# Moving weight-quantiser units between the stages of a fused two-layer kernel, and reordering each unit's steps

## The chip, the cores and the metric

One core of one Trainium2 chip. The metric is the device time of one execution in microseconds (us); lower is better. An execution before the change takes 3158.2 us (median of 3 runs, 3157.79 to 3158.3). Engines: PE multiplies matrices (PEld is its weight load), ACT is ScalarE, DVE is VectorE, POOL is GpSimd, SP issues all DMAs.

## What is computed

Two transformer layers on x (2 x 512 x 1024) with a context (2 x 1024 x 1024), in float32. Every matrix product is done as three products of high and low halves, so each operand is first split in two.

```
x = x + attention(norm(x), context)           # 32 query heads, 8 key heads, rotary, mask, projection wo
x = x + router(norm(x))                       # softmax of 64 logits, top 8, a mix of 64 bias rows
x = x + fake_quant(norm(x)) @ fake_quant(context)
x = x + w3' (silu(w1' norm(x)) * (w2' norm(x)))   # w1, w2 2752 x 1024, w3 1024 x 2752
```

w1', w2', w3' are the weights after a 4-bit quantiser: each block of 64 numbers is divided by its largest absolute value, each quotient goes to the nearest of 16 code values, and the result is multiplied back.

## The kernel before, in words

**Quantiser units.** The three weights are cut into 65 units of 128 x 1024 numbers (two are smaller), and the units are worked off beside the matrix products of four stages, on DVE, ACT and GpSimd. One unit (class Nf4): SP loads it; DVE takes the blocks' maxima and their reciprocals (max_vector, L212 to L219); GpSimd multiplies by the reciprocals (norm_gpsimd, L224); then come numbered steps. In steps 0 to 6 ACT makes a steep Relu of the normalised numbers into one of two ramp buffers (L241) and DVE adds its clipped value to the running code (L262 for step 0, else L265). In step 7 DVE subtracts the code from the numbers (L268); step 8 is empty. In step 9 ACT takes the Sign of that difference (L245) and then the first of three Prelu folds of the code (L250), steps 10 and 11 are the other folds, and after step 11 DVE makes the two final operations (L271, L273). GpSimd multiplies by the maxima (finish_gpsimd, L278) and SP stores the unit to DRAM. So NS4, the steps of a unit, is 12. Relu j waits for DVE's step j - 2, because there are two ramp buffers; the folds live in the second of them.

**Spread** (L295) gives a stage's units to its slots: the steps of all units in a row are shared out in proportion to a weight per slot. The next unit's maximum is due with step 8 of the one before (ahead), its normalisation `lag` slots later; the finish `lag` slots after the last step, the store `sync_lag` slots after that. In the front ACT and DVE do a step in the same slot; in the other stages DVE does it one slot later.

**Which units go where** (build, L2113): 34 in the front stage, 12 in attention (AT), 8 beside the projection (o_units, spread1), 11 beside the gate and down products (f_units, spread2). `chunks` counts the 128-row chunks of w1 and w2 that are quantised before the tail stage, `late_units` the units beside the projection.

**Front** (L350): keys, values and queries. 128 tiles of 24 matmuls each, with transposes between; four PSUM banks. Of a rotated tile ACT copies the result (L608), DVE makes the sine part (L658, L659), GpSimd the cosine part and the sum (L728, L731). For each pair of tiles ACT makes the high half of the next weights (L591) and GpSimd the low half (L714), two tiles ahead. Each engine works through its slot in a written order: on GpSimd the low half, then units' norms and finishes, then the rotation.

**Attention** (L821): 256 steps of scores, softmax, transposes and mixing; a unit has some 20 steps of time.

**Tail** (L1374): first the projection, 128 heads ("head" slots) of 12 matmuls; ACT splits off the high half of a head's ring buffer (L1634), GpSimd (even heads, L1912) or DVE (odd heads, L1736) the low half; SP loads a head four slots ahead. Beside it the context is turned into codes: ACT scales (L1639), GpSimd clips (L1916), DVE rounds by adding and subtracting a large constant (L1751). A second chain (class Chain) carries the router and the code product of each half of the tokens as links with hand-written slot offsets r, z, y from a base slot (64 and 128): for example z is the slot of ACT's scaling, then DVE's rounding (L1846), PE's transposes of the codes (L2060), ACT's copy, the product (L2064); y are the last transposes (L2046). Then come the gate and up products ("gate" slots, 12 matmuls) and the down products ("down" slots, twice 6 matmuls into two alternating PSUM banks that DVE adds to x, L1776). Weights of the next items are turned by PE (L2021), split by ACT (L1652) and DVE (L1764). Units of spread2 run from slot 179 to slot 337 of 392.

**SP's order at the start of the tail:** heads 0 and 1, four scales, heads 2 and 3, units 0 and 1, contexts 0 and 1, the router's weight, the expert bias, the router's bias; then slot by slot. DVE waits for the scales and for the router's three loads before its first low half:

```
            dve.wait_ge(k_ready, 1)
            dve.wait_ge(ro_in, 48)
            low(1)
            for q in range(TOTAL + 2):
```

## Time and profile before

| | us |
|---|---|
| median of 3 runs | 3158.2 |
| the profiled execution | 3158.93 |
| its span, first to last instruction | 3157.2 |
| PE busy | 2954.9 (94%) |
| DVE busy | 2311.9 (73%) |
| ACT busy | 1919.0 (61%) |
| POOL busy | 1094.0 (35%) |

The granted TensorE clock is 0.979 of full speed over the span. Busy time of PE is a union of matmuls that overlap, so it says less than the distance from one start to the next. A row of waits says who stood, whose end released it, the total in us, how often and the longest. A row of a window gives the busy time of each engine in that stretch with the count of instructions in brackets.

### The profile page before, as it was taken

The numbers are of one execution on the slowest core, as the hardware profiler recorded it, in microseconds if no ns is written. First come the engines' busy times: TensorE is split into PE (matmuls) and PEld (weight loads), VectorE is DVE, ScalarE is ACT, GpSimd is POOL, SyncE is SP. The second block draws the span as 40 slices with busy tenths as digits, with TensorE's granted clock in tenths as the row PEclk, the third lists the DMA queues.
The fourth block names the chain that finished last, engine by engine and source line by source line (L and its number), as shares of the span: only waits on it lengthen the run. The fifth ranks groups of instructions, "written<-read, shape, count | busy, mean of one in ns | idle before, by whom it ended". The sixth has DMA issues, their size and how long they took to land. (4 is left out here: it accounts for less than half of the span.)

```text
span 3157.2 us, 39853 instructions
## 1 busy us (share of the span) xinstructions
PE 2954.9 (94%) x14326; PEld 2414.3 (76%) x14336; DVE 2311.9 (73%) x3394; ACT 1919.0 (61%) x2643; POOL 1094.0 (35%) x644
## 2 busy tenths in 40 slices
PE   7989899989799999999999978998999999999999
PEld 6767687767588888888888856776786788888887
DVE  5878788788588888888888748788456666666633
ACT  4676666666488888888888756655343344444411
POOL 4626428777623333333333246543300000000000
PEclk9999999999899999999999989999999999999999
DMA  5445344343332222222222187743421232222111
GB/s 181 143 151 169 120 136 134 114 137 127 125 109 83 79 94 84 78 94 81 88 101 73 55 301 261 242 166 132 169 67 61 85 96 87 74 72 67 60 37 57
DMA packets 231108, 362.18 MB, mean 115 GB/s; under 512 B 19456, under 2 KB 114688, under 8 KB 230912
## 3 DMA queue, kind: packets, MB, share of 16 engines
q1 hardware_dynamic: 230912, 359.63, 34.4%
q8 instruction: 115, 1.88, 0.2%
q14 instruction: 81, 0.66, 0.1%
HBM read 266.90 MB, written 92.67 MB: 114 GB/s over the span
## 5 line engine op out<-in xcount | busy, mean ns | idle before, releaser
L1108 DVE CUSTOM_DVE_ANT_0 at_sc<-at_s,at_mk 128x1024 f32<-128x1024 f32 x256 | 312.0, 1219 | 100.6 <-issue 98.2
L132 PE MATMUL fr_acc<-fr_xh,fr_wh 128*128 128x512 f32 x768 | 308.8, 402 | 57.6 <-POOL fr_wl L714 52.4
L241 ACT ACTIVATE fr_nf_above<-fr_nf_raw,sharp 128x1024 f32<-128x1024 f32 (+1 forms) x238 | 258.8, 1103 | 164.6 <-POOL fr_nf_raw L224 107.0
L1123 DVE TENSOR_TENSOR at_ptl<-at_t,at_pth 128x512 fp32r<-128x512 f32 x512 | 326.5, 679 | 30.6 <-ACT at_pth L1070 30.6
L1070 ACT ACTIVATE at_pth<-at_t 128x512 fp32r<-128x512 f32 x512 | 277.4, 595 | 112.0 <-PE at_t L1170 111.3
L1060 ACT ACTIVATE at_pr<-at_sc,at_low 128x1024 f32<-128x1024 f32 x256 | 295.7, 1155 | 36.0 <-DVE at_low L1108 30.6
L133 PE MATMUL fr_acc<-fr_xl,fr_wh 128*128 128x512 f32 x768 | 305.4, 398 | 0.0
L134 PE MATMUL fr_acc<-fr_xh,fr_wl 128*128 128x512 f32 x768 | 305.0, 397 | 0.0
L1170 PE MATMUL at_t<-ident,at_pr 128*128 128x128 f32 x2048 | 267.8, 273 | 12.2 <-DVE at_ptl L1123 11.2
L1170 PEld LDWEIGHTS at_t<-ident,at_pr 128*128 128x128 f32 x2048 | 236.3, 140 | 53.9 <-issue 19.3
L265 DVE SCALAR_TENSOR_TENSOR fr_nf_val<-fr_nf_above,fr_nf_val 128x1024 f32<-128x1024 f32 (+1 forms) x204 | 246.5, 1209 | 20.4 <-ACT fr_nf_above L241 3.2
L132 PE MATMUL tl_pa<-tl_ring_h 128*128 128x512 f32 x512 | 210.0, 410 | 40.9 <-POOL tl_ring_l L1912 16.1
L1912 POOL TENSOR_TENSOR tl_ring_l<-tl_ring,tl_ring_h 128x1024 fp32r<-128x1024 f32 x64 | 162.5, 2539 | 193.6 <-ACT tl_ring_h L1634 193.5
L132 PEld LDWEIGHTS fr_acc<-fr_xh,fr_wh 128*128 128x128 f32 x768 | 148.4, 193 | 99.3 <-issue 58.0
L132 PE MATMUL at_o<-at_pth,at_vh 128*128 128x512 f32 x512 | 221.9, 433 | 0.2 <-DVE at_ptl L1123 0.2
L132 PE MATMUL at_s<-at_kh,at_qh 128*128 128x512 f32 x512 | 201.8, 394 | 11.8 <-POOL at_ql L1004 11.8
L1652 ACT ACTIVATE tl_gu<-tl_pt 128x512 fp32r<-128x512 f32 x120 | 71.7, 597 | 226.5 <-PE tl_pt L2021 226.5
L1764 DVE TENSOR_TENSOR tl_gu<-tl_pt,tl_gu 128x512 fp32r<-128x512 f32 x120 | 82.6, 688 | 169.8 <-ACT tl_gu L1652 169.2
L133 PE MATMUL tl_pa<-tl_ring_l,tl_ring_h 128*128 128x512 f32 x512 | 203.9, 398 | 0.0
L134 PE MATMUL tl_pa<-tl_ring_h,tl_ring_l 128*128 128x512 f32 x512 | 203.6, 398 | 0.0
L134 PE MATMUL at_s<-at_kh,at_ql 128*128 128x512 f32 x512 | 201.9, 394 | 0.0
L134 PE MATMUL at_o<-at_pth,at_vl 128*128 128x512 f32 x512 | 201.1, 393 | 0.0
(224 smaller groups left out, 7842.6 us busy)
## 6 DMA issues: line engine op xcount, KB each, us to landing
tl_raw<-dq SPq DMA_DIRECT2D x87, 512.0 KB, 3.6
tl_ring<-o_d SPq DMA_DIRECT2D x128, 256.0 KB, 3.2
tl_ring<-in_L_xattn_wo SPq DMA_DIRECT2D x128, 256.0 KB, 3.9
fr_nf_raw<-in_L_ffn_w SPq DMA_DIRECT2D x33, 512.0 KB, 3.6
dq<-fr_nf_val SPq DMA_DIRECT2D x33, 512.0 KB, 3.6
fr_raw<-in_L_xattn_wq SPq DMA_DIRECT2D x32, 512.0 KB, 4.5
q_d<-fr_res SPq DMA_DIRECT2D x64, 256.0 KB, 2.3
rows<-q_d SPq DMA_DIRECT2D x64, 256.0 KB, 2.7
```

Source lines behind the costliest of these rows:

```text
L132: pe.matmul(out, w[0], x[0], start=start, stop=False)
L133: pe.matmul(out, w[0], x[1], start=False, stop=False)
L134: return pe.matmul(out, w[1], x[0], start=False, stop=stop)
L241: act.activation(self.ramps[j % 2][:, w], x, ACT.Relu, bias=self.sharp[:, j:j + 1], scale=SHARP).then_inc(self.above_done.sem, 1)
L265: dve.scalar_tensor_tensor(v, above, STEPS[j], v, ALU.min, ALU.add).then_inc(self.stepped.sem, 1)
L1060: act.activation(pr[:, n % 2], sc[:, n % 2], ACT.Exp, bias=low[:, n % 2:n % 2 + 1], scale=-1.0, accum_out=sums[:, h % 2, quarter:quarter + ...
L1070: act.activation(pt[0][:, h % 2, j * HALF:(j + 1) * HALF, (n % QT) * P:(n % QT + 1) * P], t_ps[:, j], ACT.Copy).then_inc(t_hi.sem, 1)
L1108: dve.tensor_tensor_reduce(sc[:, n % 2], s_ps[:, n % 2], mk[:, bb * QT + n % QT], -1.0, -NEG, ALU.add, ALU.min, low[:, n % 2:n % 2 + 1]).t ...
L1123: dve.tensor_tensor(pt[1][sl], t_ps[:, j], f32(pt[0][sl]), ALU.subtract).then_inc(t_lo.sem, 1)
L1170: last = pe.transpose(t_ps[:, j, c, :], pr[:, n % 2, k * P:(k + 1) * P], ident[:])
L1764: dve.tensor_tensor(lo, pt[:, no % 2], f32(hi), ALU.subtract).then_inc(w_lo, 1)
L1912: pool.tensor_tensor(ring_l[:, q % 4], ring[:, q % 4], f32(ring_h[:, q % 4]), ALU.subtract).then_inc(ring_lo_p, 1)
```

## The change

The units go to 28 / 12 / 2 / 23 over the four stages. The empty step goes (11 steps): the folds follow directly on the seventh step, Sign comes last. Outside attention DVE trails ACT by one step instead of one slot (or none). The next unit's maximum is due with step 5. GpSimd does a slot's finishes ahead of its norms. In the projection the context's rounding becomes an ACT operation that adds the constant, a GpSimd clip in the shifted numbers and an ACT operation that subtracts it; the contexts come two slots later; loads at the stage's start are put into later slots; DVE's wait for the router's loads moves to slot 62. Some links of the second chain move by a slot. Beside the gate and down products, a gate slot has weight 1 and a down slot 0.3.

```diff
-NS4 = NP4 + len(FOLDS) + 2
+AHEAD = 5
+NS4 = NP4 + len(FOLDS) + 1

     def above_scalar(self, act, n, s, steps, width=D):
...
-            f = j - NP4 - 2
-            if j < NP4:
+            f = j - NP4
+            if f < 0:
...
-            if f == 0:
+            elif f < len(FOLDS):
+                scale, _, slope = FOLDS[f]
+                if f:
+                    act.wait_ge(self.above_done.sem, n * NA4 + NP4 + f)
+                else:
+                    act.wait_ge(self.stepped.sem, n * ND4 + 2 * ND4 + NP4)
+                act.activation(fold, fold if f else self.val[:, s, w], ACT.Prelu, ...)
+            else:
                 act.wait_ge(self.stepped.sem, n * ND4 + 2 * ND4 + NP4 + 1)
                 act.activation(x, x, ACT.Sign, ...)
-            if f >= 0:
-                scale, _, slope = FOLDS[f]
-                if f:
-                    act.wait_ge(self.above_done.sem, n * NA4 + NP4 + 1 + f)
-                act.activation(fold, fold if f else self.val[:, s, w], ACT.Prelu, ...)

 class Spread:
-    def __init__(self, units, weights, lag=1, sync_lag=1, ahead=8):
+    def __init__(self, units, weights, lag=1, sync_lag=1, ahead=AHEAD, norm_lag=1):
...
                 where[divmod(k, NS4)] = q
+                if k:
+                    self.late[q].append(divmod(k - 1, NS4))
+        self.late[where[divmod(total - 1, NS4)] + 1].append(divmod(total - 1, NS4))
...
-                self.norms[where[u - 1, ahead] + lag].append(u)
+                self.norms[where[u - 1, ahead] + norm_lag].append(u)

 front_stage
-        plan = Spread(len(units), [...])
+        plan = Spread(len(units), [...], lag=1, sync_lag=2)
-                for u, j in plan.steps[q]:
+                for u, j in plan.late[q]:
                     nf.step_vector(dve, u, u % 2, [j], parts[u], units[u][2])
-                    if j == 8 and u + 1 < len(units):
+                    if j == AHEAD and u + 1 < len(units):
                         nf.max_vector(dve, u + 1, ...)
...
+                for u in plan.finishes[q]:
+                    nf.finish_gpsimd(pool, u, u % 2, units[u][2])
                 for u in plan.norms[q]:
                     nf.norm_gpsimd(pool, u, u % 2, units[u][2])
-                for u in plan.finishes[q]:
-                    nf.finish_gpsimd(pool, u, u % 2, units[u][2])

 attention_stage
-        plan = Spread(len(units), [n >= UNITS_FROM for n in range(ALL - 4)], lag=2, sync_lag=6)
+        plan = Spread(len(units), [n >= UNITS_FROM for n in range(ALL - 4)], lag=2, sync_lag=6, norm_lag=2)
-                    if j == 8 and u + 1 < len(units):
+                    if j == AHEAD and u + 1 < len(units):

 Chain._batch
-        r, z, y = ..., [43 + t for t in range(QT)]
+        r, z, y = ..., [44 + t for t in range(QT)]
-        for n, (var, root) in enumerate(((2, 3), (24, 25), (40, 41))):
+        for n, (var, root) in enumerate(((2, 3), (24, 25), (41, 42))):
-                    put("dve", r[t] + 9 if n == 1 else z[t] + 4, "stats", t, n)
+                    put("dve", r[t] + 9 if n == 1 else z[t] + 5, "stats", t, n)
-                put("pe", z[t] + 2, "product", t, h)
-                put("dve", z[t] + 3, "product", t, h)
+                put("pe", z[t] + 3, "product", t, h)
+                put("dve", z[t] + 4, "product", t, h)
-            put("pe", z[t] + 1, "codes", t)
-            put("act", z[t] + 2, "codes", t)
+            put("pe", z[t] + 2, "codes", t)
+            put("act", z[t] + 3, "codes", t)

 tail_stage
-            return 1.0
+            return 1.0 if s[0] == "gate" else 0.3
-        spread1 = Spread(len(o_units), [...], lag=2, sync_lag=2)
-        spread2 = Spread(len(f_units), [...], lag=2, sync_lag=2)
+        spread1 = Spread(len(o_units), [...], lag=1, sync_lag=2)
+        spread2 = Spread(len(f_units), [...], lag=1, sync_lag=2)
+        CONTEXT_FROM = 5
         def context_slot(n):
-            return 3 + 3 * n
+            return CONTEXT_FROM + 3 * n
+        def x_slot(t):
+            return 14 + 3 * t if t < QT else 34 + 5 * t
 sync
-            for q in range(2):
+            for q in range(4):
                 load_head(q)
-            for j, v in enumerate(scales):
-                sp.dma_start(par[:, j:j + 1], ...).then_inc(par_in, 16)
-            for q in range(2, 4):
-                load_head(q)
-            for u in range(2):
-                nf1.load_early_sync(sp, u, u, o_units[u][0])
-            for n in range(2):
-                load_context(n)
-            sp.dma_start(rw, router_w).then_inc(ro_in, 16)
-            sp.dma_start(eb[:], expert_b).then_inc(ro_in, 16)
-            sp.dma_start(rb, ...).then_inc(ro_in, 16)
+            nf1.load_early_sync(sp, 0, 0, o_units[0][0])
             for q in range(TOTAL + 2):
                 if q + 4 < FIRST:
                     load_head(q + 4)
-                if 4 <= q < 4 + TT:
-                    sp.dma_start(X[:, q - 4, :], ...)
+                if q == 0:
+                    for j, v in enumerate(scales):
+                        sp.dma_start(par[:, j:j + 1], ...).then_inc(par_in, 16)
+                if q == 1:
+                    nf1.load_early_sync(sp, 1, 1, o_units[1][0])
+                if q in (2, 4):
+                    load_context(q // 2 - 1)
+                if q == 40:
+                    sp.dma_start(rw, router_w).then_inc(ro_in, 16)
+                    sp.dma_start(eb[:], expert_b).then_inc(ro_in, 16)
+                    sp.dma_start(rb, ...).then_inc(ro_in, 16)
+                for t in range(TT):
+                    if q == x_slot(t):
+                        sp.dma_start(X[:, t, :], x_tiles[t]).then_inc(x_in[t], 16)
                 for n in range(NC):
-                    if q == context_slot(n) + 2:
+                    if q == context_slot(n) + 4:
                         store_context(n)
                         if n + 2 < NC:
                             load_context(n + 2)
 scalar
+            def round_context(n):
+                act.wait_ge(ones_made, 1)
+                act.wait_ge(ctx_scaled, n + 1)
+                act.activation(rows[:, n % 2], rows[:, n % 2], ACT.Identity, bias=rounding[:, 0:1]).then_inc(ctx_rounded, 1)
+            def code_context(n):
+                act.wait_ge(ctx_clipped, n + 1)
+                if n >= 2:
+                    act.wait_ge(ctx_out[n % 2], 16 * (n // 2))
+                act.activation(codes[:, n % 2], rows[:, n % 2], ACT.Identity, bias=rounding[:, 1:2]).then_inc(ctx_coded, 1)
...
                     if q == context_slot(n):
                         scale_context(n)
+                    if q == context_slot(n) + 1:
+                        round_context(n)
+                    if q == context_slot(n) + 3:
+                        code_context(n)
 vector
-            def round_context(n):
-                dve.wait_ge(ctx_clipped, n + 1)
...
-            dve.wait_ge(par_in, 64)
...
-            dve.wait_ge(ro_in, 48)
             low(1)
             for q in range(TOTAL + 2):
+                if q == CONTEXT_FROM - 1:
+                    constants()
+                if q == plan.BASE[0] - 2:
+                    dve.wait_ge(ro_in, 48)
...
-                for u, j in of1(spread1.steps, q - 1):
+                for u, j in of1(spread1.late, q):
...
-                for u, j in of2(spread2.steps, q - 1):
+                for u, j in of2(spread2.late, q):
 gpsimd
-                pool.tensor_scalar(rows[:, n % 2], rows[:, n % 2], QMAX, 0.0, ALU.min, ALU.max).then_inc(ctx_clipped, 1)
+                pool.tensor_scalar(rows[:, n % 2], rows[:, n % 2], ROUND + QMAX, ROUND, ALU.min, ALU.max).then_inc(ctx_clipped, 1)
-                    if q == context_slot(n):
+                    if q == context_slot(n) + 2:
                         clip_context(n)
...

 build
-    chunks, late_units = 12, 8
+    chunks, late_units = 9, 2
```

## Rows read from the trace of the kernel before

**Rows 1.** The page's first line: the span and the instructions.

```profile
span 3157.2 us, 39853 instructions
```

**Rows 2.** Busy time by stage, core 0; columns as in the first line.

```profile
core 0: us, PE busy (x) PEld busy (x) DVE busy (x) ACT busy (x) POOL busy (x), PEclk, DMA share, GB/s
...
6.40:851.80 845.40, 753.19 (x3264) 612.27 (x3264) 662.15 (x722) 541.21 (x607) 509.95 (x309) 0.96 0.42 138
...
863.50:1813.00 949.50, 936.95 (x5120) 787.37 (x5120) 804.16 (x1564) 791.08 (x1314) 297.49 (x181) 1.00 0.26 87
...
1825.10:2287.00 461.90, 415.63 (x1830) 324.66 (x1836) 338.41 (x364) 264.38 (x278) 224.70 (x99) 0.95 0.62 213
2287.00:2497.00 210.00, 198.44 (x1017) 154.71 (x1022) 132.41 (x252) 73.68 (x118) 4.18 (x4) 0.98 0.21 63
2497.00:2990.00 493.00, 488.74 (x2347) 401.80 (x2346) 311.25 (x399) 217.74 (x280) 40.04 (x21) 1.00 0.25 78
```

**Rows 3.** PE in order of time in the front: start us, us, instruction.

```profile
700.00 0.39 PE L132 MATMUL fr_acc<-fr_xh,fr_wh 128*128 128x512 f32 x1
...
706.35 0.39 PE L133 MATMUL fr_acc<-fr_xl,fr_wh 128*128 128x512 f32 x1
```

**Rows 4.** What PE waited for in the front: us, times, longest.

```profile
PE fr_acc L132 <- POOL fr_wl L714: 52.4, 21, 7.3
PE fr_acc L764 <- DVE rows L670: 15.1, 1, 15.1
PE fr_acc L132 <- POOL fr_vl L720: 10.9, 1, 10.9
```

**Rows 5.** Waits of ACT and DVE in the front, same columns, whole span.

```profile
ACT fr_nf_above L241 <- POOL fr_nf_raw L224: 107.0, 25, 8.2
...
ACT fr_nf_raw L245 <- DVE fr_nf_raw L268: 94.6, 33, 5.5
...
DVE fr_nf_val L262 <- ACT fr_nf_above L241: 64.0, 22, 6.8
```

**Rows 6.** Busy time of each engine over the front's query tiles.

```profile
600.00:850.00 250.00, 216.76 (x900) 174.75 (x899) 197.72 (x205) 154.98 (x167) 182.81 (x115) 0.95 0.37 120
```

**Rows 7.** DVE in order of time in the front: three steps in a row.

```profile
703.97 3.88 DVE L265 SCALAR_TENSOR_TENSOR fr_nf_val<-fr_nf_above,fr_nf_val 128x1024 f32<-128x1024 f32 x3
```

**Rows 8.** What PE waited for in attention.

```profile
PE at_t L1170 <- DVE at_ptl L1123: 11.2, 12, 1.6
```

**Rows 9.** DVE in order of time in attention, at a unit's end.

```profile
1052.50 2.19 DVE L273 TENSOR_TENSOR at_nf_val<-at_nf_above,at_nf_val 128x1024 f32<-128x1024 f32 x1
```

**Rows 10.** What PE waited for in the projection (1813 to 2290).

```profile
PE tl_pa L132 <- POOL tl_ring_l L1912: 16.1, 5, 12.2
PE tl_pa L132 <- DVE tl_ring_l L1736: 15.9, 5, 11.3
PE tl_pa L132 <- DVE tl_X L1745: 9.2, 4, 7.3
PE tl_pc L2060 <- DVE tl_two L1846: 8.6, 3, 4.2
PE tl_pc L2046 <- DVE tl_yT L1862: 4.5, 1, 4.5
```

**Rows 11.** Order of time at the projection's start; in brackets the idle time before.

```profile
1840.28 2.36 DVE L1736 TENSOR_TENSOR tl_ring_l<-tl_ring,tl_ring_h 128x1024 fp32r<-128x1024 f32 x2 [14.96 <-DMA tl_two<-in_L_ffn_router_bias]
```

**Rows 12.** A group of ACT by line, 1815 to 2300: busy us, mean ns, idle before.

```profile
L1639 ACT ACTIVATE tl_rows<-tl_rows,tl_two 128x1024 f32<-128x1024 f32 x16 | 19.7, 1230 | 0.0
```

**Rows 13.** Busy time on the units' tile alone, gate stretch.

```profile
2497.00:2990.00 493.00, 0.00 (x0) 0.00 (x0) 142.29 (x119) 134.56 (x119) 40.04 (x21) 1.00 0.25 78
```

**Rows 14.** Groups of DVE by line, gate stretch.

```profile
L265 DVE SCALAR_TENSOR_TENSOR tl_two<-tl_two 128x1024 f32<-128x1024 f32 x66 | 80.3, 1217 | 0.9 <-ACT tl_two L241 0.3
...
L262 DVE TENSOR_SCALAR tl_two<-tl_two 128x1024 f32<-128x1024 f32 x11 | 11.6, 1056 | 0.0
```

**Rows 15.** The unit's first step on DVE in attention, by line.

```profile
L262 DVE TENSOR_SCALAR at_nf_val<-at_nf_above 128x1024 f32<-128x1024 f32 x12 | 8.2, 683 | 0.0
```

More of the change, by code:

```diff
@@ L308, in __init__ @@
         self.units, self.slots = units, slots
-        self.steps, self.maxes, self.norms, self.finishes, self.loads, self.stores = (
-            [[] for _ in range(slots)] for _ in range(6))
+        self.steps, self.late, self.maxes, self.norms, self.finishes, self.loads, self.stores = (
+            [[] for _ in range(slots)] for _ in range(7))
         where = {}
@@ L486, in weight @@
             return w
-        plan = Spread(len(units), [weight(kind, n) for kind, n, _ in ORDER])
+        plan = Spread(len(units), [weight(kind, n) for kind, n, _ in ORDER], lag=1, sync_lag=2)
         slot_of = {(kind, n, half): q for q, (kind, n, half) in enumerate(ORDER)}
@@ L1324, in _batch @@
             self._put("dve", columns_at + h + 1, "columns", b, 0, h)
-        r, z, y = [6 + 3 * t for t in range(QT)], [27 + 3 * t for t in range(QT)], [43 + t for t in range(QT)]
+        r, z, y = [6 + 3 * t for t in range(QT)], [27 + 3 * t for t in range(QT)], [44 + t for t in range(QT)]
         for t in range(QT):
             put("dve", 1 + t // 2, "stats", t, 0)
-        for n, (var, root) in enumerate(((2, 3), (24, 25), (40, 41))):
+        for n, (var, root) in enumerate(((2, 3), (24, 25), (41, 42))):
             put("act", root, "root", 0, n)
@@ L1446, in tail_stage @@
         ones = two[:, 5952:6016].bitcast(BF16)
+        rounding = words(two, 6016, 2)
         nf1 = Nf4(make_tools(ctx, nc, "t1"), sharp, buffers=nf1_buffers)
@@ L1482, in weight2 @@
                 return 0.0
-            return 1.0
-        spread1 = Spread(len(o_units), [weight1(q) for q in range(FIRST)], lag=2, sync_lag=2)
-        spread2 = Spread(len(f_units), [weight2(q) for q in range(TOTAL)], lag=2, sync_lag=2)
+            return 1.0 if s[0] == "gate" else 0.3
+        spread1 = Spread(len(o_units), [weight1(q) for q in range(FIRST)], lag=1, sync_lag=2)
+        spread2 = Spread(len(f_units), [weight2(q) for q in range(TOTAL)], lag=1, sync_lag=2)
         parts1, parts2 = ([sum(len(us[v][0]) for v in range(u % 2, u, 2)) for u in range(len(us))]
@@ L1745, in add_heads @@
                     dve.tensor_tensor(X[sl], pa[:, t], X[sl], ALU.add).then_inc(o_added, 1)
-            def round_context(n):
-                dve.wait_ge(ctx_clipped, n + 1)
-                if n >= 2:
-                    dve.wait_ge(ctx_out[n % 2], 16 * (n // 2))
-                dve.tensor_scalar(codes[:, n % 2], rows[:, n % 2], ROUND, ROUND + QMID, ALU.add, ALU.subtract).then_inc(ctx_coded, 1)
             def product(i, j):
@@ L1893, in _ @@
                     hidden_low(i, j)
-                for n in range(NC):
-                    if q == context_slot(n) + 1:
-                        round_context(n)
                 for kind, b, t, h in chain.due("dve", q):
                     link(kind, b, t, h)
-                for u, j in of1(spread1.steps, q - 1):
+                for u, j in of1(spread1.late, q):
                     nf1.step_vector(dve, u, u % 2, [j], parts1[u])
-                    if j == NP4 and u + 1 < len(o_units):
+                    if j == AHEAD and u + 1 < len(o_units):
                         nf1.max_vector(dve, u + 1, (u + 1) % 2, parts1[u + 1], parts=len(o_units[u + 1][0]))
-                for u, j in of2(spread2.steps, q - 1):
+                for u, j in of2(spread2.late, q):
                     nf2.step_vector(dve, u, u % 2, [j], parts2[u])
-                    if j == NP4 and u + 1 < len(f_units):
+                    if j == AHEAD and u + 1 < len(f_units):
                         nf2.max_vector(dve, u + 1, (u + 1) % 2, parts2[u + 1], parts=len(f_units[u + 1][0]))
@@ L1950, in _ @@
                     pool.tensor_scalar(xn[:, t % 2], xn[:, t % 2], QMAX, 0.0, ALU.min, ALU.max).then_inc(c_clip, 1)
+                for u in of1(spread1.finishes, q):
+                    nf1.finish_gpsimd(pool, u, u % 2)
                 for u in of1(spread1.norms, q):
                     nf1.norm_gpsimd(pool, u, u % 2)
[L1953 to L1954 removed]
+                for u in of2(spread2.finishes, q):
+                    nf2.finish_gpsimd(pool, u, u % 2)
                 for u in of2(spread2.norms, q):
                     nf2.norm_gpsimd(pool, u, u % 2)
[L1957 to L1958 removed]
         @block.tensor
```

36 lines of the change are left out of this document (18 added, 18 removed).

## Prediction

> **What bounds the kernel now.** The profiled execution took 3158.93 us, 0.73 above the median of 3158.2; its span is 3157.2 us [rows 1], and 1.7 us lie around it. I cut the span into its stages first [rows 2]: the front (6.4 to 851.8), attention (863.5 to 1813), the projection (1825.1 to 2287), the first gate items with the second token batch's side chain (to 2497), the gate items that carry quantiser units (to 2990), the end. PE is busy nearly everywhere, so each stage has to be held against PE's own pace. Where PE lacks nothing its matmuls start 6.35 us / 28 = 0.227 us apart [rows 3]. The front's 3072 such matmuls need 697 us and its 192 transposes some 21 (the 3264 in its row), 718 of 845.4: it loses 127 us. Attention is at its pace but for a few us. The unit-carrying gate stretch has PE busy 488.7 of 493. So the money is in the front and in the projection, and the gate stretch has nothing to give.
>
> What PE waits for there: in the front 52.4 us in 21 waits for GpSimd's low halves of the weights, one wait of 15.1 for DVE's normalised rows, one of 10.9 for GpSimd's low half of the value weights [rows 4]. The rest of the 127 is start-up and the clock: 0.96 granted on average, so part of the stage at the lower of its two levels (1.2 GHz), against 1.00 in attention [rows 2]. GpSimd is only where it surfaces. In the front ACT stood 107.0 us for the unit's normalisation and 94.6 for DVE's subtraction ahead of Sign, DVE 64.0 for the first Relu of a unit [rows 5]: the three engines stop each other at each unit's start and end, and the low half queues in order behind that. From 600 to 850, 900 matmuls are 37.5 tiles; per tile DVE was busy 197.7/37.5 = 5.27 us, GpSimd 4.87, ACT 4.13, and PE at its pace needs 24 x 0.227 = 5.45 [rows 6]. DVE would have to be 97% busy with no wait; it has waits, so PE has.
>
> **The change, part by part.** Units (65 in all) go from 34/12/8/11 to 28/12/2/23. A unit's instructions are unchanged; their order, the lag of DVE behind ACT and the empty twelfth step change.
>
> *Front, six units fewer.* Consecutive DVE steps start 3.88/3 = 1.29 us apart [rows 7]; a unit has 11 long ones (two of them the end, one the maximum) and two short, 14.3 us. With 3.1 of 12 steps per tile, units are 3.6 of the 5.27; times 28/34 that is 3.0, so DVE falls to 4.67, 86% of PE's 5.45. Steps per full query tile fall from 3.2 to 2.4. The stalls go too: the next unit's maximum moves from step 8 to step 5, with three more steps for GpSimd's normalisation (the 107.0 and the 64.0); the folds read the finished value at once and Sign comes last, after DVE has long subtracted (the 94.6); DVE trails by one step within the slot. What is late next is the end of a unit (Relu 1 shares the folds' buffer, so ACT waits about two DVE steps), and a load that is issued a slot later with its maximum sooner: about 2.5 slots for a transfer, absorbed by the four accumulator banks. Of the 52.4 I take 42, of the 15.1 13, of the 10.9 8 and 5 of the small waits: 68, and with them 15 of the 29 us that clock and unlisted gaps cost. **Front -83** (bounds -35, where GpSimd's 4.87 of 5.45 stays the limit, and -105, all but start-up).
>
> *Attention.* Same units, same lag; but the maximum now shares a slot with a step. PE already has 12 waits, 11.2 us, for DVE here, one per unit [rows 8], where a unit's end holds DVE (2.19 us for the last sum [rows 9]). A maximum plus a step is 3.0 us against 3.4 there, so a second, smaller wait per unit: **+4** (0 to +12).
>
> *Projection.* PE waits for both kinds of low halves 16.1 + 15.9 (12.2 of it the stage's first load, which stays), 9.2 at sweep ends, 8.6 for the rounded codes, 4.5 for the last transposes [rows 10]. After the first head PE stands because DVE's first low half sits behind the router bias, the last of the start's loads: 14.96 us of idle DVE [rows 11]. That wait moves to slot 62, its three loads to slot 40, ten slots ahead of their use; x tiles spread out, and unit 1 and the contexts are issued behind head loads and no longer ahead of them. Six units leave DVE (86 us), ACT (6 x 12.4 = 74) and GpSimd. The 16 context roundings leave DVE; ACT gets 32 operations like its scaling, 1.23 us each [rows 12], 39 us, less than the 74 that left it, within PE's three heads per context. If that cover goes, ACT's splits are late, up to +10. SP now holds head loads behind a context's code, but four slots ahead of PE. The codes get one slot more, which covers the 8.6. Of 42 us of waits that can go I take 36, and 10 of the half-clock (0.95 here). **Projection -46** (-25 to -60).
>
> *Second side chain.* Codes: -3. But the last transposes come a slot later and now border on the first gate that reads them: 0 to 4.5 (the row of the same wait [rows 10]), I take 4. **+1.**
>
> *Gate stretch, twelve units more.* In 493 us the units' own tile took DVE 142.3 us and ACT 134.6 [rows 13]; DVE was busy 311.3 in all [rows 2], so 164 after some 5 us of short unit work is other work. Now 164 + 5 (issue) + 23 x 14.3 = 498 of 493, 101%. ACT: 217.7 - 134.6 + 23 x 12.4 = 368, 75%. DVE becomes the bound. Weights 1 for gate slots and 0.3 for down slots put two steps in a gate slot: with 164/158 us of other work per slot about 3.6 us of DVE, against PE's 493/158 = 3.1. So DVE is 2 to 5 us behind when a down group starts, and there PE has two banks and can only cover some 1.5 us: it stands 1 to 3.5 us at each of 14 groups, 2 on average: 28 us. Queued behind late steps are DVE's adds, the low halves of weights (slack of two slots) and, on SP, weight loads behind the units' stores (slack of ten). GpSimd gets 24 more operations. In this stretch DVE's two-input step takes 1217 ns and its only slowed form is the unit's first step, 1056 [rows 14] against 683 in attention [rows 15]; 11 x 0.37 is 4 us beside 21 GpSimd operations, and I take as much for the 24 more. Of 28 + 4 a lagging DVE makes up some 2 in the slots after the last unit: **gate +30.** Below: +5, the bare excess of DVE's sum, if backlog is spread perfectly. Above: +110, if DVE gets no further than the 79% at which it was busy while it held PE up in the front (198 of 250 [rows 6]; busy alone its work is 164 + 23 x 13.6 = 477, and 477/0.79 = 603). Today PE idles 4.3 us here [rows 2] and DVE's steps hardly wait, so I stay nearer to the lower end.
>
> The Trainium skill, "SBUF — State Buffer", section "SBUF: two separate sides", says that VectorE operations with two SBUF inputs and GpSimd operations exclude each other on a shared port pair for a whole instruction. Attention's 2.19 us sum beside a GpSimd subtraction looks like it, the 1217 ns steps of the gate stretch do not. By the page every added GpSimd operation could block DVE for its length, which would put about 46 us in place of my 4 and the sum near 3106.
>
> **Sum:** -83 + 4 - 46 + 1 + 30 = -94; 3158.9 - 94 = 3065 for a profiled execution, 3064 us for the median.
>
> **Rivals.** (a) *The gate stretch hides it*, +5, and the front gives 95: 3027. For: ACT and GpSimd have room. Against: 101%. (b) *GpSimd keeps the front*: -35, so 3112. For: PE's waits name it, 89% per tile. Against: it idles on the waits that go. (c) *GpSimd blocks DVE in the gate stretch*: operations that met DVE's idle time now meet work, and each of the 24 stops DVE for its own length, 40.04/21 = 1.9 us [rows 13]: 46 in place of 4, so 3106. For: the 2.19 us row. Against: the 1217. The Trainium skill's page named above would have this one. (d) *Slower*: in the gate stretch Relu, step and fold stop each other as they do in the front, with PE directly behind DVE's adds at every down group. Its 477 us of DVE work at the projection's busy share of 338/462 = 73% [rows 2] take 651, +158 in place of +30: 3192. It decides from a share below 77% (477/617: then it eats the other stages' 124). That counts are not what the change says is no rival: they follow from two constants.
>
> **How the numbers follow.** Forecast 0.54 (3040 to 3095), (a) 0.15, (b) 0.12, (c) 0.10, (d) 0.09. The range 3015 to 3125 holds the forecast, (a), (b), (c) with their mixed bounds and leaves (d) and double mishaps out. A measurement of this kernel can tell about 0.2%, 6 us. Slower: (d) with a little, 0.10; the same: (b) and (c) together with a gate stretch at +60, 0.05; faster 0.85.
>
> **What would show it.** Front: PE's wait for the weights' low half under 15 us, the 107.0, 94.6 and 64.0 mostly gone, end near 770. Projection: no wait for the router bias, none for the codes; about 415 us long. Gate stretch: DVE above 44 of 50 busy, PE's waits for DVE's adds some 25 to 30 us in about 14 or more pieces. Wrong if the front still ends after 810, if the gate stretch grows by over 60 us, or if its waits sit on weights' low halves in place of the adds.

## The result and the profile after

After the change a run takes 3212.35 us (median of 4, 3211.61 to 3216.21) against 3158.25 (median of 4, 3157.79 to 3160.53): a ratio of 1.0166, 95% interval 1.0154 to 1.0179. The change makes the kernel 54 us slower; 94 us faster was forecast.

The windows of the profile after, cut at the first and last matmul of each stage: front, attention, projection, the rest of the side chain, the gate stretch up to the quantiser's last instruction, the end. The columns are those of [rows 2].

```profile
core 0: us, PE busy (x) PEld busy (x) DVE busy (x) ACT busy (x) POOL busy (x), PEclk, DMA share, GB/s
6.40:756.10 749.70, 730.29 (x3264) 603.80 (x3264) 577.16 (x644) 470.64 (x541) 491.24 (x298) 0.99 0.45 147
767.10:1732.60 965.50, 940.50 (x5120) 786.31 (x5120) 811.72 (x1564) 792.58 (x1313) 303.08 (x181) 1.00 0.25 85
1744.70:2192.10 447.40, 414.94 (x1836) 325.76 (x1836) 225.51 (x273) 230.59 (x245) 195.51 (x87) 0.96 0.60 205
2192.10:2398.10 206.00, 196.69 (x1023) 153.39 (x1023) 131.60 (x252) 71.08 (x115) 4.17 (x4) 0.99 0.21 64
2398.10:3050.10 652.00, 541.26 (x2383) 433.89 (x2382) 487.76 (x561) 364.46 (x419) 100.60 (x46) 0.92 0.25 79
```

The last row decides. The kernel before, cut in the same way, has this one (a little wider than the last of [rows 2]):

```profile
2493.90:2997.70 503.80, 499.54 (x2397) 410.69 (x2396) 317.89 (x408) 223.09 (x287) 41.93 (x22) 1.00 0.25 79
```

and PE waited in it, but for small gaps, for DVE's adds alone:

```profile
PE tl_pa L132 <- DVE tl_X L1776: 4.2, 5, 1.3
```

So the gate stretch grew by 148 us. DVE is busy in 487.8 of 652 us, 75%. PE's busy time grew by 42 us for no more matmuls: the granted clock fell from 1.00 to 0.92 in the stretch, so part of it ran at the lower of the two levels, 1.2 GHz. The rest of the 148 is PE standing. What PE waited for after the change, by stage (front, attention, projection, gate stretch), in us, times, longest; the line numbers are those of the kernel after:

```profile
PE fr_acc L133 <- POOL fr_wl L720: 5.4, 1, 5.4
...
PE at_t L1176 <- DVE at_ptl L1129: 23.8, 23, 2.4
...
PE tl_pa L133 <- POOL tl_ring_l L1938: 24.7, 4, 12.1
PE tl_pa L133 <- DVE tl_X L1775: 8.8, 4, 5.3
PE tl_pc L2074 <- DVE tl_two L1841: 7.2, 1, 7.2
...
PE tl_pa L133 <- DVE tl_X L1800: 64.5, 15, 7.9
PE tl_pt L2049 <- DVE tl_gu L1788: 35.3, 16, 4.6
PE tl_pa L133 <- DVE tl_dn L1788: 8.1, 5, 4.6
```

The front's 52.4 us [rows 4] are down to 5.4; attention's 12 waits [rows 8] are 23; in the projection GpSimd's low halves cost more than before [rows 10]; and in the gate stretch PE stands 64.5 + 35.3 + 8.1 = 108 us for DVE (its adds at L1800, the weights' low halves at L1788), where it was idle for some 4 before. What ACT and DVE waited for in that stretch:

```profile
ACT tl_two L250 <- DVE tl_two L268: 106.1, 23, 14.0
ACT tl_two L242 <- DVE tl_two L268: 68.1, 57, 6.9
ACT tl_two L242 <- DVE tl_two L276: 47.1, 17, 12.5
...
DVE tl_gu L1788 <- ACT tl_gu L1678: 59.6, 53, 4.3
DVE tl_X L1800 <- PE tl_pa L135: 49.7, 49, 2.4
DVE tl_dn L1788 <- ACT tl_dn L1678: 24.4, 19, 5.2
```

These waits form a ring. ACT's Relus and folds (L242, L250) wait for DVE's steps (L268; L276 is a unit's last sum), with the weights' high halves queued behind them; DVE waits for those high halves (L1678) and for PE's sums, with its steps queued behind; PE waits for DVE. Every engine has idle time, and none can use it.

### The profile page after: what moved, and what is told of

It reads as the page before. It is cut to its first block and busy times, and to the rows that moved or that the text cites. A ratio compares the mean times of both kernels' runs of the same rounds, so it can differ in the third digit from the quotient of the medians.

```text
span 3210.8 us, 39903 instructions
## 1 busy us (share of the span) xinstructions
PE 2979.2 (93%) x14336; PEld 2431.1 (76%) x14336; DVE 2291.4 (71%) x3378; ACT 1956.0 (61%) x2675; POOL 1108.9 (35%) x646
## 5 line engine op out<-in xcount | busy, mean ns | idle before, releaser
L133 PE MATMUL fr_acc<-fr_xh,fr_wh 128*128 128x512 f32 x768 | 300.9, 392 | 7.1 <-POOL fr_wl L720 5.4
L242 ACT ACTIVATE fr_nf_above<-fr_nf_raw,sharp 128x1024 f32<-128x1024 f32 (+1 forms) x196 | 215.9, 1102 | 114.7 <-DVE fr_nf_val L268 53.2
L242 ACT ACTIVATE tl_two<-tl_two,sharp 128x1024 f32<-128x1024 f32 x161 | 184.4, 1148 | 124.9 <-DVE tl_two L268 68.1
L1766 DVE TENSOR_TENSOR tl_ring_l<-tl_ring,tl_ring_h 128x1024 fp32r<-128x1024 f32 x64 | 92.4, 1444 | 198.4 <-ACT tl_ring_h L1649 198.3
L133 PE MATMUL tl_pa<-tl_dn,tl_hT 128*128 128x512 f32 x352 | 155.9, 443 | 80.9 <-DVE tl_X L1800 69.2
L268 DVE SCALAR_TENSOR_TENSOR fr_nf_val<-fr_nf_above,fr_nf_val 128x1024 f32<-128x1024 f32 (+1 forms) x168 | 201.3, 1198 | 13.7 <-ACT fr_nf_above L242 3.0
L1649 ACT ACTIVATE tl_ring_h<-tl_ring 128x1024 fp32r<-128x1024 f32 x128 | 133.9, 1053 | 124.1 <-PE tl_pa L135 79.2
```

Of the source, the lines that this page charges most:

```text
L133: pe.matmul(out, w[0], x[0], start=start, stop=False)
L242: act.activation(self.ramps[j % 2][:, w], x, ACT.Relu, bias=self.sharp[:, j:j + 1], scale=SHARP).then_inc(self.above_done.sem, 1)
L268: dve.scalar_tensor_tensor(v, above, STEPS[j], v, ALU.min, ALU.add).then_inc(self.stepped.sem, 1)
L1649: act.activation(ring_h[:, q % 4], ring[:, q % 4], ACT.Copy).then_inc(ring_hi, 1)
```

## The experiments

The theories of the gate stretch's loss. **A**: 23 units are too much work for DVE beside its evictions (the operations that take PE's results out of PSUM). **B**: the new order locks ACT and DVE together (a fold waits for DVE's step of the same slot). **C**: the weights 1 and 0.3 bunch the steps. Two more came after x1 to x4. **B'**: a unit's chain alternates between ACT and DVE in either order and sets the pace. **Port**: DVE and GpSimd stop each other.

Each of these kernels but x12 ran once. A stage whose code several of them share tells how much one run can say: with the new order and 28 units the front took 746.5 to 750.9 us in seven runs, the projection with the change's own code 447.4 to 450.2 in three, so a difference under some 5 us in a stage says little.

**x1: the new order, the old units.** "Order" stands here and below for all of the change but the number of units: the steps' order, the codes, the loads' places, the side chain's slots and the slots' weights.

```diff
-    chunks, late_units = 9, 2
+    chunks, late_units = 12, 8
```

> The new order of steps and the new placing of the context codes, but the units as they were before: 34 in the front, 12 in attention, 8 in the projection, 11 in the gate stretch. Theory A (amount: in the gate stretch VectorE has too much to do for 23 units beside the evictions): with 11 units the gate stretch is back at 493 us within 15, although the order is the new one. Theory B (lockstep: a fold on ScalarE waits for VectorE's step of the same slot, and both queues are in order): the stretch stays over 510 us with 11 units. By both the front comes to 800 to 850 us (A: 845, since the six units that left it made the gain; B: below 820, since there the order itself made part of it) and the projection to 450 to 500 us. Total 3140 to 3200 us.

3212.6 us, beside 3161.8 for the kernel before in the same session. **x2: the old order, the new units** is the kernel before with one line changed:

```diff
-    chunks, late_units = 12, 8
+    chunks, late_units = 9, 2
```

> The kernel before in every line but the numbers of units: 28/12/2/23, with the old order of steps, the old lags, the context codes as they were, and the gate stretch's steps spread evenly over its slots. A (amount): gate stretch 620 to 670 us as with the new order. B (lockstep of the new order): below 590 us. A third, C (the weights 1 and 0.3 of gate and down slots bunch the steps): also below 600 us, since here they lie evenly, and then a run of the change with even weights tells B from C. Front 760 to 800 us if the six units alone make its gain, projection 400 to 430 us.

3159.9 us. The two halves of the change are now apart (us, stages cut as above; the whole is the median for the kernel before and after, one run for x1 and x2):

| order, units | front | attention | projection | side chain | gate stretch | whole |
|---|---|---|---|---|---|---|
| old, 34/12/8/11 (before) | 845.4 | 949.4 | 461.7 | 207.1 | 503.8 | 3158.3 |
| new, 34/12/8/11 (x1) | 845.6 | 967.7 | 494.3 | 205.9 | 506.5 | 3212.6 |
| old, 28/12/2/23 (x2) | 740.8 | 950.0 | 417.0 | 207.2 | 653.7 | 3159.9 |
| new, 28/12/2/23 (after) | 749.7 | 965.5 | 447.4 | 206.0 | 652.0 | 3212.4 |

The units alone, in the old order: -104.6 in the front (more than the 45 to 85 that I had written down), -44.7 in the projection, +149.9 in the gate stretch, together nothing. The order alone, with the old units and with the new: 0 and +9 in the front, +18 and +16 in attention, +33 and +30 in the projection, +3 and -2 in the gate stretch; with the side chain's -1 these make 53 and 52 us, nearly the whole loss of 54. B falls, since 11 units in the new order take 506.5 and 23 in the old one 653.7; C falls, since x2's steps are evenly spread. A is left, and a chain through both engines that is as long in either order, B'.

These are x2's stretch, and what PE waited for in it:

```profile
2344.70:2998.40 653.70, 541.79 (x2399) 434.13 (x2398) 473.62 (x565) 365.94 (x419) 91.85 (x46) 0.93 0.26 80
```

```profile
PE tl_pa L132 <- DVE tl_X L1776: 82.0, 22, 7.9
PE tl_pt L2021 <- DVE tl_gu L1764: 26.3, 15, 3.7
```

The ring is there in the old order too: in x2's stretch ACT waits 91.2 us for DVE's steps, 71.1 for its subtraction and 62.7 for a unit's last sum, 225 in all beside 221 in the change. With 11 units in the old order the same three were 20.2, 5.7 and 12.6.

**x3: VectorE's steps halved. x4: ScalarE's steps halved.** In the gate stretch alone:

```diff
-                    nf2.step_vector(dve, u, u % 2, [j], parts2[u])
+                    nf2.step_vector(dve, u, u % 2, [j], parts2[u], D if j == 0 else 512)     # x3
-                    nf2.above_scalar(act, u, u % 2, [j])
+                    nf2.above_scalar(act, u, u % 2, [j], D if j < 2 else 512)                # x4
```

> The change, but in the gate stretch's 23 units VectorE's later steps (all but the first of a unit) work on half the columns, as does its subtraction and its two last operations; the other half of these units' values is left wrong. The waits are all kept. This takes about 23 x 9 operations x 0.6 us = 125 us off VectorE in the stretch (487 to about 365 us) and nothing off ScalarE. A (VectorE is the bound): the stretch gives back most of the 125 us and stands at 530 to 560 us. B (lockstep: a cycle through both engines): it gives back about the same, since the chain is shorter by as much. Told apart only together with the next run, in which ScalarE's work is halved instead.

> The change, but in the gate stretch's 23 units ScalarE's steps (from the third of a unit on: ramps, folds, sign) work on half the columns; the other half of these units' values is left wrong. The waits are all kept. This takes about 23 x 9 x 0.5 us = 105 us off ScalarE in the stretch (365 to about 260 us) and nothing off VectorE. A (VectorE is the bound): the stretch moves by less than 20 us. B (lockstep): it gives back over 50 us, to below 600 us.

The gate stretch of x3, then of x4:

```profile
2403.50:2972.10 568.60, 520.85 (x2384) 421.16 (x2383) 377.47 (x562) 362.75 (x419) 95.88 (x46) 0.96 0.29 91
```

```profile
2400.30:3006.70 606.40, 521.71 (x2383) 418.98 (x2382) 487.69 (x561) 278.64 (x419) 100.57 (x46) 0.96 0.27 85
```

DVE lost 110 us of work and the stretch 83; ACT lost 86 and the stretch 46. That is more than the 20 that A allows for ACT and less than B's 50, and x3's 568.6 is above A's 560. A chain through both engines is at work, and since the order plays no part, it is B' or a mixture with A.

**x5: no waits between the two engines** in these 23 units, with an edit in attention and one in the projection.

```diff
     # gate stretch, VectorE: the unit itself (raw) in place of ScalarE's ramps; no wait for above_done
-    dve.scalar_tensor_tensor(v, above, STEPS[j], v, ALU.min, ALU.add)
+    dve.scalar_tensor_tensor(v, x, STEPS[j], v, ALU.min, ALU.add)
     # gate stretch, ScalarE: the first fold reads raw; Relu and Sign wait for ScalarE's own results alone
-    # attention and projection
-        plan = Spread(..., lag=2, sync_lag=6, norm_lag=2)
-                    if j == AHEAD and u + 1 < len(units):
+        plan = Spread(..., lag=2, sync_lag=6, ahead=8, norm_lag=2)
+                    if j == 8 and u + 1 < len(units):
-        spread1 = Spread(..., lag=1, sync_lag=2)
+        spread1 = Spread(..., lag=1, sync_lag=2, norm_lag=6)
```

> The change with one edit in each of three stages, each to be read from its own stage. Gate stretch: ScalarE and VectorE do the same number of operations of the same sizes for the 23 units, but VectorE reads the unit itself instead of ScalarE's result and ScalarE the unit instead of VectorE's, so neither waits for the other in the quantiser (these units' values are therefore not the quantiser's). Theory A (the amount of work on VectorE): the stretch stays at 630 to 655 us. Theory B' (the chain of a unit that alternates between the two engines, 652/23 = 28.3 us a unit with the old order and with the new, so 17 units or so would go into a stretch of 500): the stretch falls below 580 us with the same busy times. Attention: the next unit's maximum is taken at VectorE's empty step 8 instead of with step 5; if the +17 us of the new order there come from that place, attention is back at 950 us within 4, else it stays at 966. Projection: GpSimd takes the second unit's normalisation six slots after the maximum instead of one; if GpSimd's standing before it costs the matmuls what its wait is, the projection loses 8 to 14 us of its 447, else under 4.

**x6: the codes back on VectorE, GpSimd nearly idle in the gate stretch.**

```diff
-    pool.tensor_scalar(rows, rows, ROUND + QMAX, ROUND, ALU.min, ALU.max)         # slot + 2
+    pool.tensor_scalar(rows, rows, QMAX, 0.0, ALU.min, ALU.max)                   # the scaling's slot
-    round_context, code_context on ScalarE (slot + 1, slot + 3), store at slot + 4
+    dve.tensor_scalar(codes, rows, ROUND, ROUND + QMID, ALU.add, ALU.subtract)    # slot + 1, store at slot + 2
-    nf2.finish_gpsimd(pool, u, u % 2), nf2.norm_gpsimd(pool, u, u % 2)
+    nf2.finish_gpsimd(pool, u, u % 2, BLK), nf2.norm_gpsimd(pool, u, u % 2, BLK)
```

> The change with an edit in each of two stages. Projection: the context codes are made as before (ScalarE scales, GpSimd clips in the same slot, VectorE rounds one slot later, stored two slots later); the units stay at two. The old order and old codes with two units took 417 us there, the new order and new codes 447: if the codes make the difference, the projection comes to 415 to 425 us, if GpSimd's wait for the second unit's maximum or the new order of loads does, it stays over 435. Gate stretch: GpSimd's normalisation and finish of the 23 units work on 64 of 1024 columns (the other columns stay unscaled), which takes nearly all of its 100 us away. Theory port (VectorE and GpSimd stop each other there): the stretch falls by 40 us or more; A or B': by less than 15 us.

The gate stretch of x5, then the projection and the gate stretch of x6:

```profile
2379.90:2968.70 588.80, 523.41 (x2383) 420.94 (x2382) 496.26 (x561) 361.38 (x419) 100.62 (x46) 0.96 0.27 88
```

```profile
1744.50:2177.80 433.30, 408.58 (x1836) 322.46 (x1836) 247.44 (x289) 199.01 (x213) 188.00 (x87) 0.97 0.62 212
2388.30:3013.30 625.00, 531.13 (x2381) 425.79 (x2379) 462.17 (x561) 364.41 (x419) 28.14 (x46) 0.94 0.27 83
```

Gate stretch: -63 us without the waits, though DVE was busy for 8.5 us more, so the chain is real, but 588.8 is above the 580 of B' and far below A's 630: neither alone. GpSimd: -27, between the two limits written down, and DVE's busy time fell by nearly as much (487.8 to 462.2). DVE's steps (L268) of the change and of x6, in ns min/median/max, show how:

```profile
L268 DVE SCALAR_TENSOR_TENSOR tl_two<-tl_two x138: 1160/1224/2605, 2417.2 to 3039.8; 128x1024 f32<-128x1024 f32 x138
```

```profile
L268 DVE SCALAR_TENSOR_TENSOR tl_two<-tl_two x138: 1160/1219/1228, 2407.5 to 3004.6; 128x1024 f32<-128x1024 f32 x138
```

Most steps run freely; 13 of the 138 take 2.0 to 2.6 us, each begun while a GpSimd operation ran, and with GpSimd nearly idle none does.

Attention came to 954.7 us in x5 with 15 waits (13.9 us) in place of 23; with the same edit it took 950.6 in x9 and 951.2 in x13, so the maximum beside a step is nearly all of the 16 us. In the projection the late normalisation gave 6 us and the codes on DVE 14. Both lie between the limits written down for a cause and for none, so neither is the whole of the 30.

**x9: the edits of x5 and x6 together. x13:** x9 with VectorE's later steps in the gate stretch on 512 columns, the second side chain's slots as before (z + 1, z + 2, y = 43, ...) and `lag=2` in spread1.

> The change with the edits of x5 and x6 together: in the gate stretch no waits between ScalarE and VectorE in the 23 units and GpSimd on 64 of 1024 columns (values not the quantiser's, most columns unscaled), in attention the maximum at the empty step, in the projection the codes as before and the normalisation six slots late. If the causes are separate, the gate stretch takes 652 - 63 - 27 = 562 us within 10; if they are one loss seen twice, over 575. What is then left over the 504 us of 11 units is VectorE's amount of work by itself, in order with the evictions. Projection: 447 - 14 - 6 = 427 us if separate; 417 to 424 if the codes had kept part of the wait alive. Attention 955 us.

> The kernel of x9 with two more edits. Gate stretch: VectorE's later steps of the 23 units on half the columns (about 110 us less work; values already not the quantiser's). In x9 the stretch took 546 us with no waits between the engines and a nearly idle GpSimd; if the 42 us over the 504 of 11 units are VectorE's amount of work, it comes to 504 to 515 us, if something else is left there, it stays over 530. Projection: the second side chain's slots and the finish's lag (two slots again) as before; x9 took 434.5 us where the old order took 417, with 8.0 us of it in one wait for GpSimd, which stood at a unit's finish, and 13 us at the side chain's transposes, codes and adds. If these are the rest, it comes to 413 to 422 us; if only the finish, to 426.

Attention, projection and gate stretch of x9, then projection and gate stretch of x13:

```profile
766.40:1717.00 950.60, 935.72 (x5120) 787.66 (x5120) 809.01 (x1564) 791.70 (x1313) 301.24 (x181) 1.00 0.26 86
1729.20:2163.60 434.40, 410.79 (x1830) 324.04 (x1836) 246.75 (x289) 198.66 (x212) 189.10 (x87) 0.96 0.62 211
2371.10:2917.40 546.30, 509.09 (x2381) 413.57 (x2379) 458.82 (x561) 361.59 (x419) 28.15 (x46) 0.98 0.30 95
```

```profile
1731.50:2154.40 422.90, 405.86 (x1830) 319.98 (x1836) 236.68 (x289) 198.69 (x212) 190.39 (x87) 0.98 0.63 217
2359.90:2857.70 497.80, 495.66 (x2387) 409.59 (x2386) 356.71 (x563) 360.18 (x418) 23.27 (x46) 1.00 0.34 105
```

In the gate stretch both fall below what was written, and the stretch is accounted for: 652 less 106 for both edits is 546, and with 102 us less DVE work it is 498, PE's own time, though ACT has all its work. The 106 are 16 more than the two edits apart; GpSimd's stops had grown without the waits (DVE busy 496.3 in x5 and 458.8 in x9, 37 us against 26). So over the 504 us of 11 units the ring of waits and GpSimd's stops together cost 106 and DVE's amount of work 42, taken away in this order. The shares hang on the order: halving DVE's steps with the ring still closed, in x3, gave 83.

In the projection x9 gave no more than x6 had (434.4 and 433.3), so the late normalisation added nothing once the codes were back on DVE, and 427 was missed. The side chain's slots and the finish's lag together gave 11.5 us in x13. Of the two it is the slots that show: a wait of 7.3 us at the last transposes is gone, while GpSimd stands 16.8 us for a unit's last sum in x9 and in x13 alike. GpSimd's queue in the change, in order of time, shows what that is:

```profile
1853.84 1.90 POOL L225 TENSOR_TENSOR tl_nf<-tl_nf,tl_am 128x1024 f32<-128x1024 f32 x1 [12.25 <-DVE tl_am L220]
...
1934.31 1.90 POOL L281 TENSOR_TENSOR tl_nf<-tl_nf,tl_am 128x1024 f32<-128x1024 f32 x1 [12.61 <-DVE tl_nf L276]
```

GpSimd stood for a maximum and for a unit's last sum. DVE now trails by one step, which with two units over 128 slots is several slots, while norm and finish are still due a slot or two after ACT's step, and the heads' low halves queue behind them. A finish timed from DVE's step wasn't tried; that it explains the 6 us between x13's 422.9 and the old order's 417.0 is not shown.

**x7, x8, x10, x11: the old order with fewer units in the gate stretch**, to see where its price begins.

```diff
-    chunks, late_units = 12, 8
+    chunks, late_units = 9, 8       # x7: 28/12/8/17
+    chunks, late_units = 10, 8      # x8: 30/12/8/15; x10 with AT = 14: 28/14/8/15
+    chunks, late_units = 11, 8      # x11 with AT = 16: 28/16/8/13
```

> The kernel before with its own order, codes and lags, but the units at 28/12/8/17 instead of 34/12/8/11, so six units go from the front to the gate stretch. B' (a chain of 28.3 us a unit, 17 x 28.3 = 481 us, which lies within the 504 us that the stretch took with 11 units): the stretch takes 500 to 530 us, the front 741, the whole 3050 to 3085 us. A with an even price of 12.4 us a unit ((653.7 - 503.8)/12): the stretch takes 578 us, the whole 3130 us.

> The kernel before with its own order, codes and lags and the units at 30/12/8/15. B': the gate stretch takes 500 to 510 us, the front 845 - 4 x 17.4 = 776 us, the whole 3085 to 3105 us, slower than with 28/12/8/17 by 10 to 35 us. A with an even price: the gate stretch 554 us, the whole 3140 us.

> The kernel before with its own order and the units at 28/14/8/15: two units more in attention, where the matmuls waited only 11.2 us for 12 units and VectorE was busy 804 of 950 us. Theory room (attention takes more units in VectorE's and ScalarE's free time): attention 950 to 956 us, the front 741, the gate stretch 514, the whole 3060 to 3070 us. Theory full (VectorE at 85% is past what goes in beside the matmuls, as in the gate stretch at 75%): attention 965 us or more, the whole 3075 us or more.

> The kernel before with its own order and the units at 28/16/8/13: four units more in attention. Room: attention under 965 us, the gate stretch 506 to 510 us, the whole 3055 to 3070 us. Full: attention over 985 us, the whole 3090 us or more.

| units | front | attention | projection | gate stretch | whole |
|---|---|---|---|---|---|
| 28/12/8/17 (x7) | 741.4 | 950.1 | 462.5 | 540.9 | 3091.7 |
| 30/12/8/15 (x8) | 760.0 | 950.8 | 459.0 | 513.6 | 3080.4 |
| 28/14/8/15 (x10) | 738.8 | 952.7 | 460.3 | 513.5 | 3062.0 |
| 28/16/8/13 (x11) | 740.6 | 962.3 | 460.8 | 509.6 | 3071.5 |

The gate stretch's price is a bent line: from 11 units to 15 it is 2.5 us a unit, from 15 to 17 it is 14, from 17 to 23 it is 19. x7 falls between both theories' numbers: an even price is wrong, and so is a fixed 28.3 us a unit, by which 17 units would have gone into 481 us of the 504. The front's gain is bent too: the first four units that leave it give 85 us (x8), the next two 19 (x7). x8 had 776 written down for the front, by an even 17.4 us a unit; so the whole came out below its range, and faster than x7 by 11 us where slower was expected. Attention takes two units for 2 us, though DVE is busy 832.8 of 952.7 us there, 87%; four cost 12. So no one busy share is the bend for every stage. x10 is as its expectation has it, x11 a little above its range as a whole (3071.5, 3070).

**x12: x10, timed.**

> The kernel of x10 again (the old order, 28/14/8/15), now timed against the kernel before in five rounds: 3062 us within 4, a ratio of 0.970 within 0.002 to the kernel before.

3062.5 us (median of 5) beside 3158.9: ratio 0.9693, interval 0.968 to 0.9706. It beats both kernels, by 96 us and 150 us.

## Why the prediction was wrong

**Front, -83: it came to -96.** PE's wait for the low halves fell to 5.4 us, the end to 756. But the reason was half wrong, and that the sum came so near is in part luck. The units alone give -104.6; the new order gives nothing with 34 units and takes 9 us with 28. In x1, with all 34 units, PE still waits 40.9 us for GpSimd's low halves, of the 52.4 before. I had counted the waits of [rows 5] as gone with the order. They moved: in x1 ACT waits in the front as follows.

```profile
ACT fr_nf_above L250 <- DVE fr_nf_val L268: 122.6, 34, 5.6
ACT fr_nf_above L242 <- DVE fr_nf_val L268: 67.1, 83, 3.0
ACT fr_nf_above L242 <- DVE fr_nf_val L276: 36.7, 23, 4.2
ACT fr_nf_above L242 <- POOL fr_nf_raw L225: 21.2, 13, 4.2
```

The normalisation's 107.0 are 21.2, Sign's 94.6 are 3.5, and in their place the first fold of each of the 34 units waits 3.6 us for DVE's last step: folds first means folds waiting.

**Attention, +4: it was +16,** with the second wait per unit that was forecast (23 for 12), above the upper bound of 12. The maximum beside a step is nearly all of it (x5, x9).

**Projection, -46: it was -14.** The step's first half, six units fewer, gave -45 by itself, in the old order. "Less than the 74 that left it" was the wrong test for the codes: ACT did have the room on average, but a code passes ACT, GpSimd and ACT again in four slots, and the engines waited for each other; with the codes on DVE 14 us came back. In the projection after the change:

```profile
ACT tl_codes L1666 <- POOL tl_rows L1942: 29.7, 13, 9.3
```

The side chain's slots, which were to save the codes' wait, cost most of the 11.5 that x13 gave back. The wait for the router's loads did go, and GpSimd's stand for late steps came in its place.

**Side chain, +1: -1.**

**Gate stretch, +30: +148. This is the step that failed.** It went past the prediction's own sign of being wrong, a growth of over 60 us. DVE's work was sized well: 498 us forecast with issue, 477 busy alone, 488 measured. The error is that DVE was taken to work on without a pause, 101% full, with PE losing two us at each of 14 down groups: waits between ACT and DVE, which the prediction had listed for the front, were put at nothing here. DVE reached 75%. PE's waits for its adds came in 15 pieces, about as many as forecast, but of 4.3 us, 64.5 in all and as long as 7.9; the weights' low halves, to which I gave two slots of slack, cost 43 more, and the clock's fall, for which the sum had no term, another 42. In their place the runs show a ring of waits between ACT and DVE (63 us when it alone is opened, in x5), GpSimd's stops of DVE (27, x6; 106 for both, x9), and DVE's amount of work in what is left (42). I had two higher prices in hand, the 79% and rival (d)'s 73%, and stayed near the lower end since DVE's steps hardly waited with 11 units. But that row was taken at 63% busy (317.9 of 503.8), on the flat part of the line; the line turns steep between 15 units, 72%, and 17, 74%.

**The rivals.** (d), at 0.09, had the direction and the mechanism: Relu, step and fold do stop each other (63 us), with PE directly behind. Its stretch grew by 158 us, the measured one by 148. That the size came so near is in part luck: the 73% was borrowed from the projection, and no run shows why DVE should stop at that share; without the ring and GpSimd's stops it was busy 84% of the stretch (x9). Its whole, 3192, is 20 us short, since the other stages together gave 94 and not 124. (a) fell, since the gate stretch hides little past 15 units. (b) fell: GpSimd's waits went with the units. (c) was partly so: taking nearly all of GpSimd's work away gave 27 us for all 46 operations, where (c) had 46 us for the 24 new ones and I had 4 for them.

What such a meeting looks like: a step of 2.60 us began 0.39 us after a GpSimd normalisation of 1.91, and another normalisation, which began 0.16 us after a step of 1.16, took 2.75.

```profile
2760.07 1.16 DVE L268 SCALAR_TENSOR_TENSOR tl_two<-tl_two 128x1024 f32<-128x1024 f32 x1
...
2788.84 2.60 DVE L268 SCALAR_TENSOR_TENSOR tl_two<-tl_two 128x1024 f32<-128x1024 f32 x1
```

```profile
2760.23 2.75 POOL L225 TENSOR_TENSOR tl_two<-tl_two,tl_am 128x1024 f32<-128x1024 f32 x1 [11.55 <-DVE tl_am L220]
...
2788.45 1.91 POOL L225 TENSOR_TENSOR tl_two<-tl_two,tl_am 128x1024 f32<-128x1024 f32 x1 [11.56 <-DVE tl_am L220]
```

The Trainium skill, "SBUF — State Buffer", section "SBUF: two separate sides", says that of a VectorE operation in a two-port mode or with two SBUF inputs and a GpSimd operation that reads SBUF the one that starts first gets the shared pair of ports for the whole instruction, and the other blocks. The trace agrees for these pairs, in both directions.

(c)'s price, a whole GpSimd operation each time, was too high. 23 of the 46 took 2.3 to 2.8 us in place of 1.9, each begun 0.16 us after a unit's step on DVE: there GpSimd waited. DVE's busy time is 26 us above that of x6, while the 46 add up to 100.6 us.

Over the stages, what the units gave in the front and the projection, 149 us, is what they took in the gate stretch, 150; the order's 52 came on top, where the forecast had counted the order as a gain.

## To carry to other kernels

An engine that works through its queue in order, serves the matmuls and also waits for another engine did not fill up to 100% here: 75% in the gate stretch. Don't price added work by the free time left. A busy share taken from another stage is no safe price either (attention took 87% with almost no loss): expect a bent line, flat at first and then steep, and measure two or three amounts to find the bend. When a wait is taken away by reordering, write down who waits at the new place, and time every operation from the engine that feeds it, not from the slot of the first in the chain. Move work in small amounts to where the line is still flat: two units from the front to attention cost 2 us there and saved 21, while the reordering as a whole cost 52 to 53 us with the old units and with the new.

## Of the hardware, not expected

The granted clock made the loss larger: the same matmuls of the gate stretch had PE busy 499.5 us at a granted 1.00 and 541.3 at 0.92, after waits of up to 7.9 us. The stops between DVE and GpSimd fall on few operations but in full: 13 of 138 steps take 2.0 to 2.6 us in place of 1.22, where the mean of 1.33 hides it. DVE's adds of matmul sums (L1800) never took more than 0.69 us in the same stretch, GpSimd at work or not.
